# Attention and a gated feed-forward on one core: gate and up made in their own row, from a second buffer of tokens

## What is computed

```python
xn = layernorm(x)
qkv = xn @ qkv_w + qkv_b
attn = softmax(einsum('bnhd,bmhd->bhnm', q, k) * 16 ** -0.5)
attended = einsum('bhnm,bmhd->bnhd', attn, v) @ proj_w + proj_b
wg, wu, wd = w_gate / 127, w_up / 127, w_down / 127
gate, up = xn @ wg.T, xn @ wu.T
out = x + attended + (silu(gate) * up) @ wd.T
```

## Time and profile before

| | us |
|---|---|
| three runs, median (lowest to highest) | 593.06 (589.63 to 597.27) |
| profiled execution, its span | 591.3 |
| TensorE busy in that span | 561.3 |
| VectorE, ScalarE, GpSimd busy | 466.7, 415.9, 303.2 |

### The profile page before, as it was taken

One profiled execution on the slowest core, in us unless ns is written; L12 is line 12 of the kernel. 1 busy time (PEld: TensorE's weight loads), 2 busy tenths in 40 slices (PEclk: granted clock), 3 DMA queues, 4 the chain that ended last, 5 costly groups with the idle time before them and its releaser, 6 DMA issues.

```text
span 591.3 us, 13815 instructions
## 1 busy us (share of the span) xinstructions
PE 561.3 (95%) x4844; PEld 335.8 (57%) x4844; DVE 466.7 (79%) x603; ACT 415.9 (70%) x572; POOL 303.2 (51%) x285
## 2 busy tenths in 40 slices
PE   7697899999999999999999999999999999998896
PEld 7455346555655556555655557555665556564453
DVE  5858668898878888888878888888878887688742
ACT  3735666788758876788758876788758876587562
POOL 3146533756466554856466554856466552355220
PEclk9989989999999999999999999999999999899999
DMA  8890439361872549361872549361762449330201
GB/s 268 229 238 15 108 131 220 64 147 36 227 193 50 125 143 231 72 145 35 222 192 51 125 142 231 72 148 32 223 190 52 91 144 220 86 55 8 68 2 38
DMA packets 55120, 74.91 MB, mean 127 GB/s; under 512 B 5680, under 2 KB 28208, under 8 KB 55088
## 3 DMA queue, kind: packets, MB, share of 16 engines
q1 hardware_dynamic: 55088, 74.47, 49.7%
HBM read 40.90 MB, written 33.03 MB: 125 GB/s over the span
## 4 chain that ended last, share of the span: by engine, by line
PE 76%; DMA 9%; DVE 5%; issue 4%; ACT 4%; SPq 1%; POOL 1%; ACTq 0%; DVEq 0%; POOLq 0%
PE dense L1269 20%; PE o_bank L1243 18%; PE st_bank L1210 13%; PE dense L1313 11%; PE s_bank L1227 10%; DVE neg_max L990 2%; PE dense L1253 2%; DMA k_spread<-qk_parts 2%; DMA out<-resid 2%; DMA resid<-in_L_attn_x 2%; ACT probs L829 1%; DMA probs<-in_L_attn_qkv_w 1%; PE dense L1382 1%; SPq L589 1%; DMA xn_blocks<-x_turned 1%
## 5 line engine op out<-in xcount | busy, mean ns | idle before, releaser
L990 DVE TENSOR_REDUCE neg_max<-s_bank 128x2 f32<-128x1024 f32 x250 | 304.9, 1220 | 73.0 <-PE s_bank L1227 71.4
L829 ACT ACTIVATE probs<-st_bank 128x1024 f32<-128x1024 f32 x250 | 256.5, 1026 | 123.4 <-PE st_bank L1210 121.4
L1243 PE MATMUL o_bank<-probs,v_ones 128*32 128x512 f32 x1024 | 138.3, 612 | 0.1
L1210 PE MATMUL st_bank<-q_stack,k_stack 50*128 50x512 f32 x500 | 118.0, 465 | 6.7 <-ACT probs L829 6.3
L1210 PEld LDWEIGHTS st_bank<-q_stack,k_stack 50*128 50x128 f32 x500 | 47.9, 185 | 132.9 <-ACT probs L829 78.9
L1227 PE MATMUL s_bank<-k_stack,q_stack 48*128 48x512 f32 x500 | 109.4, 431 | 7.6 <-DVE neg_max L990 4.1
L736 POOL TENSOR_TENSOR hid_tl<-gated,hid_th 128x512 fp32r<-128x512 f32 x48 | 61.6, 1284 | 34.5 <-ACT hid_th L929 34.5
L730 POOL TENSOR_TENSOR gated<-gated,hid 128x512 f32<-128x512 f32 x48 | 61.6, 1283 | 26.8 <-DVE gated L1012 13.4
L1227 PEld LDWEIGHTS s_bank<-k_stack,q_stack 48*128 48x128 f32 x500 | 47.7, 186 | 28.8 <-DVE neg_max L990 13.8
L1269 PE MATMUL dense<-xn_tl,w_uh 64*128 64x512 f32 x176 | 62.4, 394 | 0.0
L1269 PE MATMUL dense<-xn_tl,w_gh 64*128 64x512 f32 x176 | 62.4, 394 | 0.0
(11 more groups left out here) (152 smaller groups left out, 900.7 us busy)
## 6 DMA issues: line engine op xcount, KB each, us to landing
q_stack<-q_spread SPq DMA_DIRECT2D x64, 192.0 KB, 4.8
k_stack<-k_spread SPq DMA_DIRECT2D x64, 192.0 KB, 5.3
q_spread<-qk_parts SPq DMA_DIRECT2D x16, 512.0 KB, 4.9
k_spread<-qk_parts SPq DMA_DIRECT2D x16, 512.0 KB, 5.8
q_spread<-qk_parts SPq DMA_DIRECT2D x16, 256.0 KB, 5.3
k_spread<-qk_parts SPq DMA_DIRECT2D x16, 256.0 KB, 2.0
resid<-in_L_attn_x SPq DMA_DIRECT2D x16, 256.0 KB, 4.1
out<-resid SPq DMA_DIRECT2D x15, 256.0 KB, 2.2
```

The lines of the kernel that those rows point to most:

```text
L829: nc.scalar.activation(probs[:, s % 2, 2 * half:2 * half + 2, :], transposed_bank(row, s, half)[:, :, :], ACT.Exp, scale=SCALE).then_inc(e ...
L990: nc.vector.tensor_reduce(neg_max[:, g % 2, :, NT * pair + qt], score_bank(row, half)[:, :, :], AX_X, ALU.max, negate=True).then_inc(max_d ...
L1210: done = nc.tensor.matmul(transposed_bank(row, s, half)[:, r, :], k_stack[rows, pair, P * kt:P * (kt + 1)], q_stack[rows, pair, :], start= ...
L1243: done = nc.tensor.matmul(o_bank[32 * j:32 * (j + 1), :], v_ones[:, kt, 8 * (g // 2) + 2 * j + g % 2, :], probs[:, (s - 1) % 2, j, :], sta ...
```

## The change

Gate and up of a row are made in that row: pairs 0 and 1 in steps 0 and 2, pairs 2 to 5 in steps 7 to 10; down moves to steps 13 and 15, q and k of index 1 to steps 11 and 12, v 0 to step 14. The tokens get a second pair of buffers (`tokens_of`), so their split waits for no pair any more; qk_parts becomes a single one, whose halves wait for each other's spread. Row 0 (`ROW0`) and row 7 (`LAST`) get tables of their own; the loop covers two rows at a time, rows 1 to 4. Statistics move to steps 3 to 5, `normalise` to (6, 2), the turns to steps 11 and 12.

The prologue makes no pairs. SyncE loads w_up, w_down, proj_w and the biases behind the first spread and the first stack; raw_u lies in the places of gated and v_part, and v_ones is set at the start, on GpSimd. In the prologue q1, k1 and v0 come ahead of the leading scores, w_up, w_down, the first group's maxima and proj_b's addition (`vbias`) among them and behind them. ScalarE converts w_up and w_down, copies each transposed part twice (whole and high), and GpSimd subtracts; VectorE did these conversions and subtractions before. The squares of the lows are products of each 128 x 128 part with itself (`gram`: twelve of w_g after v0 in the prologue, twelve of w_u and twelve of w_d in row 0), of whose sum VectorE takes the diagonal. TensorE branches after step 1 of row 0. SyncE loads the third group's maxima ahead of q1 and k1, and takes the turn of tokens in two pieces around the next row's first maxima.

```diff
--- before.py
+++ after.py
 STEADY = [
-    (0, 0, "up", 4, 0, (2,)), (0, 0, "gate", 4, 0, (0,)),
-    (1, 0, "v", 1, 0, (1, 2)),
-    (2, 0, "up", 5, 0, (1,)), (2, 0, "gate", 5, 0, (0,)), (2, 0, "max", 1, 0, (2,)),
-    (3, 0, "proj", 0, -1, (2, 1)),
-    (4, 0, "q", 0, 1, (0, 2)),
-    (5, 0, "k", 0, 1, (1, 0)),
-    (6, 0, "proj", 1, -1, (2, 1)), (6, 0, "max", 2, 0, (0,)),
-    (7, 0, "q", 1, 1, (2, 0)),
-    (8, 0, "k", 1, 1, (1, 2)),
-    (9, 0, "down", 0, 0, (0, 1)),
-    (10, 0, "down", 1, 0, (1, 2)), (10, 0, "max", 3, 0, (0,)),
-    (11, 0, "up", 0, 1, (1,)), (11, 0, "gate", 0, 1, (0,)),
-    (12, 0, "up", 1, 1, (2,)), (12, 0, "gate", 1, 1, (1,)),
-    (13, 0, "up", 2, 1, (0,)), (13, 0, "gate", 2, 1, (2,)),
-    (14, 0, "up", 3, 1, (1,)), (14, 0, "gate", 3, 1, (0,)), (14, 0, "max", 0, 1, (2,)),
-    (15, 0, "v", 0, 1, (2, 1)),
+    (0, 0, "up", 0, 0, (1,)), (0, 0, "gate", 0, 0, (0,)),
+    (1, 0, "v", 1, 0, (2, 1)),
+    (2, 0, "up", 1, 0, (0,)), (2, 0, "gate", 1, 0, (2,)), (2, 0, "max", 1, 0, (1,)),
+    (3, 0, "proj", 0, -1, (1, 0)),
+    (4, 0, "q", 0, 1, (2, 1)),
+    (5, 0, "k", 0, 1, (0, 2)),
+    (6, 0, "proj", 1, -1, (1, 0)), (6, 0, "max", 2, 0, (2,)),
+    (7, 0, "up", 2, 0, (2,)), (7, 0, "gate", 2, 0, (1,)),
+    (8, 0, "up", 3, 0, (0,)), (8, 0, "gate", 3, 0, (2,)),
+    (9, 0, "up", 4, 0, (1,)), (9, 0, "gate", 4, 0, (0,)),
+    (10, 0, "up", 5, 0, (2,)), (10, 0, "gate", 5, 0, (1,)), (10, 0, "max", 3, 0, (0,)),
+    (11, 0, "q", 1, 1, (0, 2)),
+    (12, 0, "k", 1, 1, (1, 0)),
+    (13, 0, "down", 0, 0, (1, 2)),
+    (14, 0, "v", 0, 1, (0, 1)), (14, 0, "max", 0, 1, (2,)),
+    (15, 0, "down", 1, 0, (0, 2)),
+]
+ROW0 = [
+    (1, 0, "v", 1, 0, (2, 1)),
+    (2, 0, "max", 1, 0, (1,)),
+    (3, 0, "up", 0, 0, (1,)), (3, 0, "gate", 0, 0, (0,)),
+    (4, 0, "q", 0, 1, (2, 1)),
+    (5, 0, "k", 0, 1, (0, 2)),
+    (6, 0, "up", 1, 0, (1,)), (6, 0, "gate", 1, 0, (0,)), (6, 0, "max", 2, 0, (2,)),
+] + [c for c in STEADY if c[0] >= 7]
+LAST = [c for c in STEADY if c[0] <= 3] + [
+    (4, 0, "up", 2, 0, (2,)), (4, 0, "gate", 2, 0, (1,)),
+    (5, 0, "up", 3, 0, (0,)), (5, 0, "gate", 3, 0, (2,)),
+    (6, 0, "proj", 1, -1, (1, 0)), (6, 0, "max", 2, 0, (2,)),
+    (7, 0, "up", 4, 0, (2,)), (7, 0, "gate", 4, 0, (1,)),
+    (8, 0, "up", 5, 0, (0,)), (8, 0, "gate", 5, 0, (2,)),
+    (10, 0, "max", 3, 0, (1,)),
+    (11, 0, "down", 0, 0, (0, 1)),
+    (12, 0, "down", 1, 0, (1, 2)),
 ]
 FIRST_IN_ORDER = [
     (0, 0, "xn", 0, 1), (0, 0, "xn", 1, 1), (1, 0, "q", 0, 1), (1, 2, "k", 0, 1),
     (2, 0, "wgate", 0, 1), (2, 0, "wgate", 1, 1), (2, 0, "wgate", 2, 1),
...
+    (4, 0, "q", 1, 1), (5, 0, "k", 1, 1), (6, 0, "v", 0, 1),
+    (12, 1, "wup", 0, 1), (12, 1, "wup", 1, 1), (12, 1, "wup", 2, 1),
+    (13, 2, "max", 0, 1),
+    (13, 2, "wdown", 0, 1), (13, 2, "wdown", 1, 1), (13, 2, "wdown", 2, 1),
+    (15, 2, "vbias", 0, 1),
 ]
-SQUARES_AFTER = (("wdown", 2), ("k", 1), ("max", 0))
-DECISION_AFTER = ("v", 0)
-STATS_AT = ((8, 1), (9, 1), (9, 2), (10, 1))
-AVERAGE_AT = (10, 2)
+BRANCH = 2
+STATS_AT = ((3, 1), (4, 1), (5, 1), (5, 2))
+AVERAGE_AT = (6, 2)
-TURN_AT = ((13, 1), (14, 1))
-ROW1_TURN_AT = ((0, 1), (0, 2))
+TURN_AT = ((11, 1), (12, 1))
+ROW1_TURN_AT = ((14, 1), (15, 1))
 def rows_of(engine, step):
...
-    with engine.Fori(1, ROWS - 2) as b:
+    with engine.Fori(1, ROWS - 3, 2) as b:
         step(Row(b, 1))
+        step(Row(b + 1, 2))
-        xn_t = [sb(f"xn_t{i}", [P, KC, TOK], F32R) for i in "hl"]
-        qk_parts = [sb(f"qk_parts{i}", [P, 2, 2, TOK], F32R) for i in range(KC)]
+        xn_t = [[sb(f"xn_t{i}{n}", [P, KC, TOK], F32R) for i in "hl"] for n in range(2)]
+        qk_parts = sb("qk_parts", [P, 2, 2, TOK], F32R)
+        def tokens_of(row, offset):
+            return xn_t[(row.like + offset) % 2]
...
                     raw_weight(2, raw_g.bitcast(I32).rearrange("p (k n) -> p k n", n=C),
                                w_gate.rearrange("(k p) n -> p k n", p=P))
+                    sp.wait_ge(dense_done, count(row, any_chunk, kind="xn", index=1))
+                    load_x(1)
+                    spread_heads(row, "q", 0)
+                    spread_heads(row, "k", 0)
+                    heads_spread(row, 0)
+                    load_stack(row, 0)
                     raw_weight(3, raw_u.bitcast(I32).rearrange("p (k n) -> p k n", n=C),
                                w_up.rearrange("(k p) n -> p k n", p=P))
+                    load_stack(row, 1)
                     raw_weight(4, raw_d.bitcast(I32).rearrange("p (k n) -> p k n", n=HID),
                                w_down.rearrange("(k p) n -> p k n", p=P))
...
             nc.gpsimd.memset(k_stack[:, :, :].bitcast(F32), 1.0).then_inc(ones_ready, 1)
+            nc.gpsimd.memset(v_ones[:, :, :, :], 1.0).then_inc(v_ones_ready, 1)
+            def turned_low(row, chunk):
+                kind, i = chunk[2:4]
+                w, cols = weight_place(kind, i)
+                pool.wait_ge(w_full, (0 if kind == "wup" else 3) + i + 1)
+                pool.wait_ge(act_free, count(row, freed_by_act, chunk))
+                full, high = turned[kind, i], w[0][cols].bitcast(F32)
+                apart = "p (k n) -> p k n"
+                nc.gpsimd.tensor_tensor(w[1][cols], full.rearrange(apart, k=2), high, ALU.subtract).then_inc(up_down_low, 1)
+            def projection_weights():
+                pool.wait_ge(v_bias_in, 16)
+                nc.gpsimd.tensor_copy(v_bias_rows[:, :, :], v_bias[:, :].unsqueeze(2).broadcast_to([P, KC, P])
+                                      ).then_inc(v_bias_wide, 1)
+                low_of_weights(4, w_p[1][:, :, :], raw_p, w_p[0][:, :, :])
...
                 if row.like == 0 and s < 2:
-                    act.wait_ge(squares_done, 3)
+                    act.wait_ge(w_low_pool, 2)
+                    act.wait_ge(dense_done, count(Row(-1, -1), any_chunk, kind="vbias", index=0))
+                elif kind in TURNED:
+                    w, cols = weight_place(kind, i)
+                    nc.scalar.activation(halves(turned[kind, i]), bank, ACT.Copy).then_inc(w_full, 1)
+                    nc.scalar.activation(w[0][cols], bank, ACT.Copy).then_inc(act_free, 1)
-            def square_lows(n):
...
...
+            def sum_of_diagonal():
+                dve.wait_ge(gram_done, 1)
+                nc.vector.tensor_tensor(diagonal[:, :], o_bank[:, 0:P], ident[:, :], ALU.mult).then_inc(diagonal_done, 1)
+                dve.wait_ge(diagonal_done, 1)
+                nc.vector.tensor_reduce(low_squares[:, :], diagonal[:, :], AX_X, ALU.add).then_inc(squares_done, 1)
+                        if row.like == 0 and (s, slot) == (0, 2):
+                            sum_of_diagonal()
+                        if row.like == 0 and (s, slot) == (1, 0):
+                            decide()
...
+            def gram(w, first, last):
+                low = [w[1][:, :, :].rearrange("p k n -> p (k n)")[:, tile(t)] for t in range(KH * C // P)]
+                for t, part in enumerate(low):
+                    done = nc.tensor.matmul(o_bank[:, 0:P], part, part, start=first and t == 0,
+                                            stop=last and t == len(low) - 1)
+                return done
+                    if row.like == 0 and s == 1:
+                        sum_squares()
+                        pe.wait_ge(exact_known, 1)
+                    if row.like == 0 and s == 0:
+                        pe.wait_ge(up_down_low, 6)
+                        gram(w_u, False, False)
+                        gram(w_d, False, True).then_inc(gram_done, 1)
             step(Row(-1, -1), False)
-            pe.wait_ge(exact_known, 1)
+            step(Row(0, 0), False, range(BRANCH))
             flag = pe.value_load(all_exact[0:1, 0:1], min_val=0, max_val=1)
```

286 lines of the change are left out of this document (141 added, 145 removed), and 4 rows, old and new, of the table FIRST_IN_ORDER.

## The result

The changed kernel took 638.8 us (median; 637.5 to 641.2) against 592.3 for the kernel before (589.6 to 597.3): a ratio of 1.078, 95% interval 1.073 to 1.084. The forecast was 590. Its profiled execution has a span of 639.4 us.

A forecast was written before the change was run, and what follows sets the result against it. It took TensorE, busy 561 of 591 us, as the bound; 44.5 (row 0's start) + 73.0 + 336.1 + 68.2 + 57.5 (rows 0, 1 to 5, 6, 7) + 10.25 (tail) = 589.6, forecast 590, range 578 to 602.

The forecast's parts named there:

- First scores and start of row 0: Prologue: first scores at 24.9 us, 19.4 us to the last maximum, row 0 starting at 44.5 instead of 54.05.
- the late bound of 48: Start of row 0: forecast at 44.5 us, with a range of 41 to 48.
- the squares, 4: Row 0, step 0: twenty-four products of w_u and w_d ahead of step 1's scores, taken as 4 us.
- twice that: Row 0's squares: 3.7 us at 0.154 each, and twice that if no weight load hides.
- The third rival: Slow clock stays through prologue into row 0: transposes and squares at twice their time, 6 us more, 596; chance 0.1.
- at nothing: Parts said to cost nothing: the second token buffer, the single qk_parts and the other bank numbers.
- GpSimd's lateness of 0.7 a row: Middle rows, steps 7 to 10: GpSimd's queue behind normalising costs 0.7 us a row, 3.5 in five rows.
- slack of 0.7 comes back in each step: Rows 1 to 5: recovered slack was the reason to take 0.7 us, the middle between 0 and 1.4.
- The second rival: GpSimd bounds steps 7 to 10, idle for a late residual: 3.4 us a row, 605.8 in all; chance 0.12.
- another 2 us: Within the second rival: GpSimd idle at (9,0) for the residual, pairs 4 and 5 behind it, another 2 us.
- the half of the old surplus: Row 6: had lost 3.1 us to the residual wait; half taken back, giving 68.2 (66.5 to 70.5).
- the four pairs: Row 7: four pairs moved from the prologue, 4 x 0.87 = 3.5 us, in a row of 57.5 (54 to 60.5).

The follow-up runs named there:

- e7: The changed kernel without the 24 products that square the low parts of w_up and w_down in row 0's step 0: 629.0 us.
- e10: As e9, with the low parts of w_up and w_down squared on ScalarE in the prologue instead of by TensorE products in row 0: 605.3 us.
- e13: As e11, but with a loop over one row and ScalarE's token copies (as e14) instead of rows written out: 593.6 us, 1.003 of the kernel before.
- e11: As e10, with the normalising started at step 12 instead of 13: 600.6 us, 1.008 of the kernel before.
- e9: As e5, with every engine's loop written out and normalising moved to step 13 (turns at 15, SyncE's order to suit): 610.9 us.
- e4: The changed kernel with extra products of zeros as fillers, behind w_gate's squares and each of the twelve leading scores: 634.9 us.
- e8: As e6, with every engine's loop over two rows written out, so that no engine jumps back: 634.3 us.
- e6: As e5, with statistics moved to steps 2 to 4 and normalising from step 6 to step 4: 650.6 us.
- e14: The changed kernel with a loop over one row: next tokens always in the second buffer, copied into the first by ScalarE: 621.0 us.
- e5: The changed kernel with only the bias additions to the residual moved, from steps 8 and 9 to 11 and 12: 617.0 us.
- e12: The kernel before with its one-row loop written out for every engine, nothing else: 605.9 us, 1.021 of the kernel before.
- e2: The kernel before with a loop body of two rows run twice and row 5 written out: 609.8 us against 592.8.

## Why the prediction was wrong, by its own steps

**First scores and start of row 0: sizes off.** The first score came at 25.97 (said 24.9). From it to the end of the twelfth maximum it was 21.8 us (said 19.4, though the terms listed, 14.8, 1.2 and 3, come to 19.0): VectorE stood 2.1 us at w_up's twelve transposes and 3.8 around the group maximum and w_down's (1.2 and 3 were said), since twelve take 2.8 us at half clock; and two turns of tokens, 0.7 each, stood among the maxima. Row 0 started at 48.8, past the late bound of 48.

**Row 0, 81.3 for 73.0: the squares, 4, were too small, and the clock was in the wrong place.** The bound of "twice that" was right: the 24 products at half clock hold TensorE for 5.3 us (53.36 to 58.67), and without them step 0 falls by 5.6 (e7; row 0 by 5.7 in e10). The third rival, the slow clock carried into row 0, came true: the granted clock in row 0 is 0.85, against 0.95 before. The forecast had taken the reduction as the bound of the leading scores and let the clock cost nothing. Its price in steps 1 and 2 is 4.0 us (e13 against e11). The runs account for row 0 against e13's 69.3: 2.9 us go with the backlog (e9, 78.4), 5.7 with the squares (e10, 72.8), 3.5 with the clock (e13; step 3 gives 0.7 of the 4.0 back). The Trainium skill, "TensorE: Matmul & The Clock Gate", section "HAM oscillation — how this bites in real kernels", was the warning. The trace agrees with it on the fall: TensorE waits 3.53 us for the first stack, and the granted clock is 0.50 from the first score on. That it stays at 0.50 up to row 0, with TensorE busy 16.8 of 22.8 us, and e4's fall under gapless work are not told by that section.

**Rows 1 to 5, 366.8 for 336.1: the loop at nothing, GpSimd's lateness too small, and a late residual on top.**

- *The loop wasn't costed.* The change lists a second token buffer, which stood "at nothing"; but buffers in turn need a body of two rows. That is 1214 products and as many weight loads for TensorE, twice what the earlier trace rows has in a row. The prediction read the data's queues and never the instructions' two. The jump cost row 2 some 10.5 us (e8 against e6: 12.4), and with the loads came late transfers. The Trainium skill, "Runtime: NRT & Kernel Launch", section "Instruction fetch mechanics", has a rule that was passed over: TensorE's instruction memory holds 2048 instructions, refilled in blocks of 16 KiB, and a taken branch to a target outside the current window of two such blocks waits for a fetch.
- *GpSimd's lateness of 0.7 a row was 1.9.* e14, without loads, has rows of 68.65 where e13 has 66.8. The list of GpSimd's work was right, though its terms add up to 21.5 us and not 21, in a stretch of about 22; and so was the sum for the first pair: 0.95 us of waiting at `hid_th` where some 1 was said. What failed is "slack of 0.7 comes back in each step". From the normalising on GpSimd had no gap left (none from 371.26 to 386.96 in e14's row 4), and ScalarE waited for it 0.99, 0.29, 0.61 and 0.58 us in that row. Some 1.0 us of it is the normalising's (e5 against row 6), the rest comes with the additions.
- *A late residual adds some 2 us on top.* Rows take 66.8 us with neither (e13), 67.4 with loads and the normalising's part of the backlog (e5), 68.65 with the whole backlog and no wait for the residual (e14), and 70.9 where GpSimd also waits 0.8 to 0.9 us for it (rows 1 and 4 of the changed kernel). With GpSimd full, that wait has nowhere to go. TensorE idles behind it, the clock dips (0.72 from 402 to 408 us in row 4), and steps 10 and 11 grow from 8.5 to 10.5 us. That the residual is late in rows with loads is shown for the kernel before, written out (e12); here only e14's rows without loads speak for it.

**The second rival** named the place (steps 7 to 10) and the mechanism, GpSimd idle for a late residual with pairs behind it, at 2.9 to 3.4 us a row. Rows 1 and 4 lost about 4.3 against rows of 66.6 before. Some 2.3 of them come with waits of 0.84 and 0.94 us for the residual, and that is the rival's own "another 2 us", though from a shorter wait than it had: GpSimd's waits for the residual fell from 37.1 us to 7.0. The other 2.0 are there without such a wait (e14): the work's own time on GpSimd.

**Row 6, 70.7 for 68.2:** the half of the old surplus that was said to come back didn't; with the additions later it is 66.4 (e5). The old surplus itself points to the loads, which the prediction hadn't read, though no run takes them out of that row alone: row 6 of the kernel before is written out behind the loop, nine packets of instructions are loaded in it, and its residual's second half is added 43.3 us into the row instead of 41.1 to 41.5.

**Row 7, 61.7 for 57.5:** the four pairs were sized within 1.3 us (58.8 in e5 and e13). The rest is the backlog: the last low part ended at 611.5 and down waited for it, at half clock.

```profile
611.67 1.65 PE L1334 MATMUL dense<-w_dh,hid_th 64*128 64x256 f32 x12 [1.38 <-POOL hid_tl L779]
```

**Right:** the single `qk_parts` and the bank numbers cost nothing that shows (e13's rows are as short as the old ones); the tail of 10.25 measured 10.1; row 0 did start earlier, by 5.3 us.

**Left open:** why the stall at the jump is 11.4 us in the changed kernel (5.4 to 12.1 in others with its loop) and 3.4 in e2; why row 3 is the longest of the rows written out (in e9, e10, e11 and e12 alike); how a few packets delay a transfer; and when the clock rises again in row 0.
